# The 88 blocks of the far counts, between the pieces of the last eight expert steps instead of behind them

## What is computed

```
x = layernorm(x)                                  # M = 8192 rows of 128
h = (x @ W_gat)                                   # 16 numbers a row
e = leaky_relu(a_src[src] + a_dst[dst])           # 524288 edges and a loop for each node
alpha = exp(e - max over dst) / sum over dst
agg = segment_sum(h[src] * alpha, dst)            # scores of 4 experts after a layernorm
w = softmax of the two best scores of each row
for ei in range(4):
    hh = gelu(x @ W1[ei] + b1[ei])                # 128 -> 256
    out += g[ei] * (hh @ W2[ei] + b2[ei])         # 256 -> 128, g from w
```

## Time and profile before

| | us |
|---|---|
| median of 3 runs | 1210.77 (1210.64 to 1213.56) |
| the profiled execution, its time | 1209.07 |
| its span, first to last instruction | 1207.3 |
| expert stage on PE | 470.2 to 769.6 |
| far counts on PE | 769.6 to 933 |
| the four parts and the last outputs | 940 to 1207.3 |

### The profile page before, as it was taken

One profiled execution on the slowest core, in us unless ns is written; L12 is line 12 of the kernel. 1 busy time (PEld: TensorE's weight loads), 2 busy tenths in 40 slices (PEclk: granted clock), 3 DMA queues, 4 the chain that ended last, 5 costly groups with the idle time before them and its releaser, 6 DMA issues. The chain is left out here.

```text
span 1207.3 us, 18290 instructions
## 1 busy us (share of the span) xinstructions
PE 832.1 (69%) x5404; PEld 695.1 (58%) x5404; DVE 916.9 (76%) x3061; ACT 439.6 (36%) x1069; POOL 613.5 (51%) x553
## 2 busy tenths in 40 slices
PE   0000299999999997988999999999999242323130
PEld 0000178888888885766777777888888132222030
DVE  7999967677888856979699800388888748989877
ACT  1019378775545533543555445200000403030203
POOL 2000000004777760057777777788888777875004
PEclk9999999899999987998999999855555555555555
DMA  7000011112222211121222221000000020606001
GB/s 241 0 0 1 20 36 43 42 43 46 47 59 46 43 8 8 57 73 45 62 79 62 61 79 10 9 7 7 7 7 7 10 48 9 217 9 214 17 22 35
DMA packets 73032, 55.41 MB, mean 46 GB/s; under 512 B 32531, under 2 KB 65684, under 8 KB 72981
## 3 DMA queue, kind: packets, MB, share of 16 engines
q1 hardware_dynamic: 56132, 48.71, 12.7%
q0 software_dynamic: 16384, 5.54, 5.4%
q10 hardware_dynamic: 464, 0.59, 0.1%
HBM read 36.64 MB, written 17.76 MB: 45 GB/s over the span
## 5 line engine op out<-in xcount | busy, mean ns | idle before, releaser
L551 POOL DMA_INDIRECT sb_arena<-table,sb_arena x384 | 465.3, 1212 | 186.2 <-issue 116.7
L535 POOL DMA_INDIRECT sb_late<-lists,sb_window_at x128 | 128.0, 1000 | 316.4 <-ACT sb_window_at L861 274.7
L1276 DVE TENSOR_TENSOR sb_late<-sb_far_lo,sb_iota_lo 128x1792 bf16<-128x1792 bf16 x88 | 96.2, 1093 | 102.2 <-PE ps_four L726 97.5
L726 PE MATMUL ps_four<-sb_late 128*128 128x64 bf16 x1232 | 158.8, 301 | 4.6 <-DVE sb_late L1278 0.6
L726 PEld LDWEIGHTS ps_four<-sb_late 128*128 128x128 bf16 x1232 | 141.7, 143 | 21.5 <-DVE sb_late L1278 16.3
L699 PEld LDWEIGHTS ps_four<-sb_we,sb_arena 128*128 128x128 f32 x1024 | 119.1, 191 | 27.1 <-issue 27.1
L699 PE MATMUL ps_four<-sb_we,sb_arena 128*128 128x128 f32 x1024 | 131.3, 281 | 0.0
L690 PE MATMUL ps_H<-sb_x2nT,sb_we 128*128 (+1 forms) x512 | 124.2, 387 | 0.0
L884 ACT ACTIVATE sb_arena<-ps_H,sb_be_c 128x256 f32<-128x256 f32 x256 | 106.7, 471 | 28.9 <-PE ps_H L690 27.1
L633 PE MATMUL ps_four<-sb_arena 128*128 128x256 f32 x128 | 35.5, 402 | 118.2 <-DVE sb_var L1136 118.2
L690 PEld LDWEIGHTS ps_H<-sb_x2nT,sb_we 128*128 128x128 f32 x512 | 94.9, 195 | 10.9
(11 more groups left out here) (237 smaller groups left out, 1511.7 us busy)
## 6 DMA issues: line engine op xcount, KB each, us to landing
outputs<-sb_arena SPq DMA_DIRECT2D x24, 512.0 KB, 2.7
sb_arena<-outputs SPq DMA_DIRECT2D x12, 1024.0 KB, 5.4
sb_arena<-in_adj SPq DMA_DIRECT2D x32, 256.0 KB, 2.8
sb_arena<-table,sb_arena POOLq DMA_INDIRECT x384, 2.8
sb_x2nT<-in_L_ffn_edge_index SPq DMA_DIRECT2D x8, 512.0 KB, 7.7
sb_xs<-in_x SPq DMA_DIRECT2D x32, 128.0 KB, 2.2
out_x<-sb_xs SPq DMA_DIRECT2D x16, 256.0 KB, 2.5
sb_late<-lists,sb_window_at POOLq DMA_INDIRECT x128
```

Of the source, the lines that this page charges most:

```text
L535: pool.indirect_dma_start(bk.bitcast(i32)[:, p * WINDOW:(p + 1) * WINDOW], None, lists, bass.IndirectOffsetOnAxis(ap=window_at[:, p:p + 1] ...
L551: pool.indirect_dma_start(rows[:, g, c, o, :], None, table[0:M, :], bass.IndirectOffsetOnAxis(ap=idxT[:, at:at + 1], axis=0), bounds_check ...
L726: last = nc.tensor.matmul(ps_F, hot_lo[k][:, :, c], hot_hi[k][:, :, c], start=(first and c == 0), stop=(end and c == FB - 1))
L1276: V.tensor_tensor(hot_lo[k], far_lo[:, bass.ds(b * FB, FB)].unsqueeze(1).to_broadcast([P, P, FB]), iota_lo[:, :, :], ALU.is_equal)
```

## The change

The last eight expert steps (24 to 31) are taken out of the loop of `IDX_AFTER`. They run as `counted(g, p)`: the same `experts`, which now calls `between(piece)` behind each of its six pieces. `between` issues 2, 2, 2, 2, 2 and 1 blocks of the far counts, 11 in a step, 88 in all. Step 32's outputs come behind the last block. No instruction of another engine changes, and PE's matmuls are the same ones in another order. A step has an odd number of blocks, so the buffer is taken from the parity of `p * 11 + n`.

```diff
-        IDX_AFTER = ((1, 3, 0), (3, 4, 1), (4, 6, 2), (6, GROUPS // 2, None))
+        COUNTS_FROM, PIECES = 12, (2, 2, 2, 2, 2, 1)
+        GROUP_BLOCKS = sum(PIECES)
+        IDX_AFTER = ((1, 3, 0), (3, 4, 1), (4, 6, 2), (6, COUNTS_FROM, None))
...
                             last.then_inc(s["hh_in_psum"], 1)
+                            between(3 * k + e % 2)
...
                         last.then_inc(s["eo_in_psum"], 1)
+                        between(3 * k + 2)
...
-            experts(GROUPS, 0, True)
...
-            counts(0, 0, True, False)
-            counts(1, 1, False, False)
-            with pe.Fori(1, FARCOLS // FB // 2 - 1) as j:
-                counts(2 * j, 0, False, False)
-                counts(2 * j + 1, 1, False, False)
-            counts(FARCOLS // FB - 2, 0, False, False)
-            counts(FARCOLS // FB - 1, 1, False, True)
+            def blocks_of(g, p):
+                base = (g - 2 * COUNTS_FROM) * GROUP_BLOCKS
+                def between(piece):
+                    for n in range(sum(PIECES[:piece]), sum(PIECES[:piece + 1])):
+                        at = base + n if isinstance(base, int) else None
+                        counts(base + n, (p * GROUP_BLOCKS + n) % 2, at == 0, at == FARCOLS // FB - 1)
+                return between
+            def counted(g, p):
+                experts(g, p, True, blocks_of(g, p))
+            counted(2 * COUNTS_FROM, 0)
+            counted(2 * COUNTS_FROM + 1, 1)
+            with pe.Fori(COUNTS_FROM + 1, GROUPS // 2 - 1) as j:
+                counted(2 * j, 0)
+                counted(2 * j + 1, 1)
+            counted(GROUPS - 2, 0)
+            counted(GROUPS - 1, 1)
+            experts(GROUPS, 0, True)
             pe.wait_ge(s["eo_used"], TILES)
             pe.wait_ge(s["far_added"], 1)
```

More of the change, by code:

```diff
@@ L342, in build @@
         tab_t = table[0:M, :].rearrange("(g u q) c -> g q u c", u=2, q=P)
-        IDX_AFTER = ((1, 3, 0), (3, 4, 1), (4, 6, 2), (6, GROUPS // 2, None))
+        COUNTS_FROM, PIECES = 12, (2, 2, 2, 2, 2, 1)
+        GROUP_BLOCKS = sum(PIECES)
+        assert (GROUPS - 2 * COUNTS_FROM) * GROUP_BLOCKS == FARCOLS // FB
+        IDX_AFTER = ((1, 3, 0), (3, 4, 1), (4, 6, 2), (6, COUNTS_FROM, None))
         FIRST, LOOP_FROM, LOOP_TO, END = -2, 6, GRAPHS - 2, GRAPHS + 5
@@ L681, in _, with no_counts, experts @@
             obank = [bank_T[:, :], bank_A[:, :]]
-            def experts(g, p, outs):
+            def no_counts(piece):
+                pass
+            def experts(g, p, outs, between=no_counts):
                 more = not isinstance(g, int) or g < GROUPS
```

## The result

The changed kernel takes **1249.21 us** (median, 1241.43 to 1250.84) against 1212.16 for the kernel before in the same session: ratio **1.0295, 95% interval 1.0254 to 1.0336**. The profiled execution took 1250.84 us with a span of 1249.1.

The account below looks back on a forecast made before the run. PE alone was taken to set 692.9 to 934.4, expert steps then counts. Terms -16.0 (mutual wait, stretch end) + 2.4 (type changes) + 36 (clock) = +22.4 us, carried to the median: 1233.2 us, range 1205 to 1256.

Parts of the forecast that it names:

- rival 3: In the mix PE still waits for DVE at each second block, 16 us more: +38, 1249 us; chance 0.05.
- The clock: Counts lower PE's clock over the mixed expert pieces: 72 us if low throughout, half of it taken, 36 us loss.
- long enough to bring it up in their later part: Output pieces in the mix, 2.6 us or 5.1 low, were to bring the clock back up before they end.
- stay down over the hidden pieces: Once down, the clock stays low over hidden-layer pieces of 0.9 us (1.8 low), shorter than 4 us of dense work.
- Rival 2: The clock stays down for nearly all the mix, output pieces restoring it not or only at their end: +58, 1269; chance 0.10.
- Counts without the mutual wait: In the mix PE and DVE stop waiting for each other: 88 blocks take 147.8 us against 163.5.
- the end of the stretch: Step 32's outputs now stand between the last block and line 741: about 1.0 us in place of 1.3.
- Changes between bf16 and fp32: 48 times an fp32 weight load follows a bf16 count block: 0.05 us each, 2.4 us loss; bounds nothing to 19 us.
- a low share of 0.8: Upper end of the forecast's share of mixed expert work at the low clock, 0.2 to 0.8; its times 1211 to 1256.
- rival 1: The clock holds through the mix, leaving only the gain: -16 to -13.6, 1195 to 1197, counted up to 1211; chance 0.19.
- What moves no time: DMA, SP and POOL instructions stay unmoved, no store waits, gathers fit; line 741 to the end stays 272.9 us.
- the last gather should again end near 1103.8: Gathers beside DVE's 88 blocks: the last ends as before, 14 us ahead of ACT's read at 1118.1.

Follow-up runs that it names:

- fine_48: Changed kernel with 48 blocks mixed, cut into 2 to 5 count matmuls behind hidden-layer matmuls and output pairs, 40 blocks behind step 32: 1253.59 us, ratio 1.0356 to before.
- after_ones: Changed kernel with one count block behind each of the six pieces, 48 mixed, 40 behind step 32's outputs: 1218.40 us, ratio 1.0033 to the kernel before.
- after_inner: Changed kernel with one block behind each half step's first hidden and output pieces, none behind the second hidden piece, 32 mixed: 1214.16 us, ratio 0.999 to before.
- after_cont_wide: Changed kernel with the counts' 64 moving columns side by side and streamed twice into 128 PSUM columns: 1416.88 us, ratio 1.1646 to the kernel before.

## Why the prediction was right, and where it was not

The forecast, slower by 22.4 us with a range of 1205 to 1256, has the right sign and, for the loss, the right cause; the measured 1249 lies in the upper part. It is also the time that the prediction gave to its rival 3, so the number alone doesn't tell the two apart; the waits do. The checksum's matmul came at 976.7 instead of "about 957", 19.9 us later. That divides into four terms.

- **The clock, mis-sized.** 36 us were forecast, half of 72; it was 50.8, or 0.71 of it (+14.8). The half was a choice, which no row bore out, and that it came near enough for the range is in part luck. The size of the full loss was right: most pieces have one of two lengths, hidden 0.88 and 1.78 us, bias 0.75 and 1.39, outputs 1.89 and 3.57 (start to start; those in between, as the 1.39 at 702.54, have a change of the clock in them), so near doubling holds for bias and outputs, too. The step that failed is "long enough to bring it up in their later part": the outputs ran at the low clock for 60.5 of 62.6 us. The clock came back only at their end or in the counts behind them, as the timeline from 708.80 to 715.74 shows, and the high time went to counts, which have no use for it, and to hidden pieces. Nor does it stay down over the hidden pieces as reasoned; they were low for 28.6 of 42.6 us. The 4 us of dense work that brought the clock back in the earlier trace rows were the right scale, but a low output piece with its bias is 5.0 us long and the clock fell before it: the return takes nearly the whole piece. Rival 2's condition (back "only at their end") was thus true of the outputs; what kept the time under its 1269 is that a part of the hidden pieces, 14.0 us, ran at the high clock.
- **Counts without the mutual wait, right.** 16.0 were forecast with the end of the stretch, 13.9 measured (+2.1 in the time). Count blocks keep 1.7 us at either clock. Rival 3 is out: PEld's wait for DVE is gone.
- **Changes between bf16 and fp32, not a cost** (-2.4). Ahead of fp32 nothing shows (3.35 us for two blocks from 699.19 to 702.54, ahead of a hidden piece, against 3.36 in the earlier trace rows; twelve places at no cost in fine_48). Nor are there 48 such places: 31 count stretches stand ahead of a hidden piece in fp32, 17 ahead of the bias matmuls, which are bf16 like the counts. Ahead of the bias two blocks take 3.49 us (703.93 to 707.42), and 3.46 to 3.49 wherever they stand there, at either clock. These 0.11 us in 17 places, 1.9 us, are nearly all of the 2.1 above. So the size was about right, for another reason than the one given.
- **A shift not forecast**, +5.4: step 24 already began later in this profile. It comes ahead of the changed instructions and goes with a lower clock there, as the windows of 420 to 470 and 540 to 560 show.

Together 14.8 + 2.1 - 2.4 + 5.4 = 19.9. Two small slips of the sums moved nothing: a low share of 0.8 gives 1255 and not 1256, and rival 1 has line 741 from 918 on, not 919.

**Rival 1**, the clock holds, is refuted in the mix of the change (0.66 in the window 725 to 757 with PE busy for 32.00 of 32.00 us). The rule of the Trainium skill (TensorE: Matmul & The Clock Gate, section "Why this matters for your kernels") that the prediction weighed, that idle gaps take the clock down, doesn't cover this case: here it fell without one. The same section has the clock swing with thin matmuls, where its remedy is to have no wait for a DMA between them; in this trace it swings though PE waits for none.

**What moves no time.** From the checksum on it was 272.4 us against 272.9, as forecast. But "the last gather should again end near 1103.8" is wrong: it ends at 1065.1.

```profile
1064.15 1.00 POOL L554 DMA_INDIRECT sb_arena<-table,sb_arena  x1 [0.30 <-issue]
```

In place of the 7.95 us in the earlier trace rows the last one takes 1.00. The stretch is longer and DVE's blocks are thinner in it, so 190 gathers fit in at 1171 ns each where it had been 149 at 1316; 64 are left behind the checksum instead of 105. It made the cover larger: the reader, ACT's L968, starts at 1159.93.

## What to carry to other kernels

Before work is woven into a stretch in which PE is the bound, compare what both kinds need of the clock: indifferent work that lowers it should stay together, behind the work that pays for it. If two engines hand buffers to each other in turn, try a third buffer before a new order; here it gave the whole gain, 14.8 us, without the loss. And when a mix must be, keep whole dense pieces: cutting 48 blocks finer tripled the low time. Where a matmul's time doesn't go with the clock, look at how its moving operand lies in memory.

## What the runs showed of the hardware that was not expected

- **Evenly diluted work was worse for the clock than solid stretches.** 48 blocks in solid stretches of 1.7 us left 25.4 us of expert work at 1.2 GHz, in stretches of 0.2 to 0.6 us 77.9 us, with PE busy all the time in both.
- **The one-row bias matmuls pay nearly double, too** (0.82 and 1.46 us for three), and in after_ones and after_inner each fall of the clock in the mix showed in the output piece right behind them.
- **A moving operand with columns 28 bytes apart costs 1.8 to 1.9 ns a column at either clock**, which is why the counts don't care for the clock. With the same 128 columns side by side, 14 matmuls took 0.92 us at the high clock and 1.50 at the low one (after_cont_wide), in place of 3.28. The Trainium skill (SBUF — State Buffer, section "Specifications (TRN2)") says that full bandwidth needs at least two accesses to a 16-byte line and that each crossing has a penalty; one access a line is what the spaced columns do, and the trace agrees.
- **DVE's bf16 write with a stride of 128 bytes took 4.15 us instead of 0.62**, 6.7 times as long, for the same 128 x 896 numbers.
